# Graph attention and routed FFN on one core: POOL's gathers take their cue from TensorE's steps

## What is computed

```
xn   = layernorm(x);  xp = (xn @ W) as 4 heads x 64
alpha = leaky_relu(a_src[src] + a_dst[dst])
w    = softmax of alpha over the edges of each target (with a loop edge)
x    = x + elu(segment_sum(xp[src] * w, dst) + bias)
xn   = layernorm(x);  r = xn @ wr + br
y    = (gelu(xn @ w1 + b1) @ w2 + b2) * r    for the K = 6249 nodes of largest r, in one choice over all nodes
x    = x + xn  (every node), + y (chosen nodes)
```

## Time and profile before

| | us |
|---|---|
| median of 3 runs | 3182.54 (3172.71 to 3183.56) |
| the profiled execution's own time | 3182.05 |
| its span, first to last instruction | 3180.3 |
| PE busy | 2095.3 (66%) |
| POOL busy | 1596.4 (50%) |
| DVE busy | 1597.0 (50%) |
| ACT busy | 722.8 (23%) |
| mean granted clock of TensorE | 0.789 of full speed |
| DMA | 365.42 MB, 115 GB/s over the span |

### The profile page before, as it was taken

One profiled execution on the slowest core, in us unless ns is written; L12 is line 12 of the kernel. 1 busy time (PEld: TensorE's weight loads), 2 busy tenths in 40 slices (PEclk: granted clock), 3 DMA queues, 4 the chain that ended last, 5 costly groups with the idle time before them and its releaser, 6 DMA issues.

```text
span 3180.3 us, 39382 instructions
## 1 busy us (share of the span) xinstructions
PE 2095.3 (66%) x10886; PEld 1777.2 (56%) x10887; DVE 1597.0 (50%) x3933; ACT 722.8 (23%) x1899; POOL 1596.4 (50%) x1675
## 2 busy tenths in 40 slices
PE   8646766657666666676676666766657567676675
PEld 6535655546556555565555555655556555565564
DVE  7654545444454454544544545445445454454556
ACT  5301221212212222122121221221212212122123
POOL 3465545455454554545545545455455454554530
PEclk9867878777787787777877878778778787787788
DMA  7643333333333333333333333333333333333329
GB/s 244 189 123 106 106 104 105 102 105 107 102 106 104 105 104 104 105 103 108 103 103 102 110 99 106 104 105 101 105 103 105 106 102 102 99 109 101 107 72 318
DMA packets 216050, 365.42 MB, mean 115 GB/s; under 512 B 62102, under 2 KB 151346, under 8 KB 216019
## 3 DMA queue, kind: packets, MB, share of 16 engines
q0 software_dynamic: 77488, 214.85, 25.7%
q1 hardware_dynamic: 124434, 136.80, 14.0%
q10 hardware_dynamic: 14096, 13.41, 1.2%
HBM read 326.04 MB, written 38.89 MB: 115 GB/s over the span
## 4 chain that ended last, share of the span: by engine, by line
PE 62%; issue 33%; DVE 3%; DMA 0%; ACT 0%; DVEq 0%; ACTq 0%; SPq 0%
PE ag_ps L939 28%; PE h_ps L909 15%; PE y_ps L922 10%; PE lk_ps L890 3%; PE tr_ps L898 2%; PE ag_ps L831 2%; PE ag_ps L952 1%; DVE base L1442 1%; DVE st_b L1056 0%; PE y_ps L924 0%; DMA node_rows<-base 0%; DVE rows L1250 0%; PE tr_ps L854 0%; PE xl_ps L854 0%; DVE rows L1046 0%
## 5 line engine op out<-in xcount | busy, mean ns | idle before, releaser
L637 POOL DMA_INDIRECT rows<-node_rows,ends x1613 | 1555.6, 964 | 1393.8 <-PE ag_ps L939 908.7
L909 PE MATMUL h_ps<-xnT,w1s 128*128 128x128 f32 x3136 | 488.5, 286 | 818.1 <-issue 818.0
L939 PE MATMUL ag_ps<-rows,oh 128*128 128x260 f32 x3322 | 946.2, 454 | 31.2 <-issue 23.2
L909 PEld LDWEIGHTS h_ps<-xnT,w1s 128*128 128x128 f32 x3136 | 421.5, 199 | 820.1 <-issue 808.7
L939 PEld LDWEIGHTS ag_ps<-rows,oh 128*128 128x128 f32 x3322 | 759.0, 232 | 180.9 <-issue 33.6
L1300 DVE SCALAR_TENSOR_TENSOR base<-steps_of_rows 128x256 f32 (+1 forms) x98 | 42.0, 429 | 1365.8 <-ACT steps_of_rows L790 1365.8
L1250 DVE TENSOR_TENSOR rows<-rows,xl_ps 128x768 f32<-128x768 f32 (+2 forms) x685 | 495.6, 793 | 29.1 <-ACT xl_ps L750 18.1
L721 ACT COPY xnT<-tr_ps 128x256 f32<-128x256 f32 x98 | 36.7, 374 | 1428.9 <-PE tr_ps L898 1337.3
L922 PE MATMUL y_ps<-w2s,hT 128*128 128x256 f32 x1568 | 355.4, 379 | 1.6 <-ACT hT L731 1.6
L922 PEld LDWEIGHTS y_ps<-w2s,hT 128*128 128x128 f32 x1568 | 297.4, 190 | 42.5 <-issue 1.8
L1212 DVE TENSOR_TENSOR oh<-xl_ps,dloc 128x2176 f32<-128x2176 f32 x98 | 236.9, 2418 | 0.0
(11 more groups left out here) (206 smaller groups left out, 1380.0 us busy)
## 6 DMA issues: line engine op xcount, KB each, us to landing
dbc<-dst SPq DMA_DIRECT2D x97, 544.0 KB
rows<-node_rows,ends POOLq DMA_INDIRECT x1613
selfr<-node_rows SPq DMA_DIRECT2D x98, 130.0 KB
base<-in_x SPq DMA_DIRECT2D x14, 896.0 KB, 5.8
base<-in_x SPq DMA_DIRECT2D x49, 256.0 KB
ffn_rows<-yb ACTq DMA_DIRECT2D x96, 128.0 KB, 1.7
node_rows<-base SPq DMA_DIRECT2D x13, 910.0 KB, 5.8
out<-base SPq DMA_DIRECT2D x3, 1024.0 KB, 9.2
```

Source lines behind the costliest of these rows:

```text
L637: pool.indirect_dma_start(out=rows[:, b, t, :], out_offset=None, in_=table, in_offset=bass.IndirectOffsetOnAxis(ap=ends[:, b, t, 0:1], axi ...
L909: last = nc.tensor.matmul(h_ps[:, m * P:(m + 1) * P], w1s[:, c, m * P:(m + 1) * P], xnT[:, c, :], start=(c == 0), stop=(c == DC - 1))
L939: product = nc.tensor.matmul(ag_ps[b][:, 0:ROW], oh[:, b, t, :], rows[:, b, t, :], start=(t == 0), stop=False)
```

## The change

POOL no longer waits for `freed` of block w-2. In block w (from w = 1 on) it waits, ahead of gather 4, for the look-ups of block w (`lk_ok`); ahead of gathers 8, 11 and 13, for the three groups of sums of block w-1 (`freed[0]`, `freed[1]`, `freed[2]`); and ahead of gather 16, for the second FFN layer of block w-4, which PE does behind the sums of block w-1 (`y_ok`). Gather 0 waits for `ends` alone. That the products of block w-2 are done before gather 0 of block w follows from the wait ahead of gather 13 in block w-1. POOL's loop has its first two turns written out instead of one. Apart from this, SP waits for `y_ok` and loads the "ffn" rooms ahead of the first store of `out` rather than behind it.

```diff
+    LOOKED_UP, SUMMED, SECOND_LAYER = 4, (8, 11, 13), TILES - 1
...
             sp.wait_ge(y_st[1], 16 * (PAIRS - 1))
+            sp.wait_ge(y_ok, NW)
+            load_free("ffn")
             for c, (first, count, _) in enumerate(ends_with):
...
-                if c == 0:
-                    sp.wait_ge(y_ok, NW)
-                    load_free("ffn")
...
+            def follow(w, t):
+
+                if t == LOOKED_UP:
+                    wait_apart(pool, (lk_ok, w + 1))
+                for k in range(GROUPS):
+                    if t == SUMMED[k]:
+                        wait_apart(pool, (freed[k], w))
+                if t == SECOND_LAYER and known(w, 4):
+                    wait_apart(pool, (y_ok, w - 3))
+
...
                 for t in range(last):
-                    if known(w, 2) and t % FREED == 0:
-
-                        wait_apart(pool, *([(ld_ends[b], 32 * (i + 1))] if t == 0 else []), (freed[t // FREED], w - 1))
+                    if known(w, 2) and t == 0:
+                        wait_apart(pool, (ld_ends[b], 32 * (i + 1)))
+                    if known(w, 1):
+                        follow(w, t)
                     gather(t, gath[b])
+                if known(w, 1):
+                    follow(w, last)
...
-            two_by_two(pool, PAIRS, window, last_peeled=True)
+            two_by_two(pool, PAIRS, window, last_peeled=True, first_peeled=2)
```

## The result

| | before | after |
|---|---|---|
| median, us | 3181.79 (3172.71 to 3183.56, 4 runs) | 2711.39 (2703.0 to 2718.25, 4 runs) |
| ratio, 95% interval | | 0.8528 [0.8502, 0.8555] |
| profiled execution, us | 3182.05 | 2703.0 |
| its span | 3180.3 | 2701.2 |
| granted clock | 0.789 | 0.844 |

Faster by 470 us, where 202 were forecast. The time lies outside the range (2740 to 3200) and nearest to the rival "the crawl nearly goes" (2738).

What follows compares the result with a forecast made beforehand. The bound was a ring of POOL's gathers and PE's work, 30.8 us a block; 93 periods at -2.1 us give -195, start -5 and end -2.4, so 3182 - 202 = 2980 us, range 2740 to 3200.

Steps and rivals of the forecast that it cites:

- the crawl nearly goes: Rival: almost nothing left for PE after its slow stretch; -4.7 us a block, 2738 us; chance 0.13.
- the crawl: PE's slow stretch while POOL gathers: one pair of weight load and matmul per 2.1 us, against 0.12 before.
- The ring and the stock: Steady block: 21.0 us gathers, 2.8, then 7.0 of PE's work; during gathers PE lives on some 60 held pairs.
- another cause, tied to PE's place: Rival: PE's slowness comes from its place, not from held pairs; no change, about 3180 us; chance 0.13.
- one pause, and inner waits that cost nothing: POOL idles some 7 us ahead of gather 4; later waits end before POOL arrives, 0.1 us a block.
- -5.4 + 0.1 + 2.8 + 0.4 = -2.1: Us a block: POOL's earlier start, later waits, PE's pairs left, turn wholly behind the slow stretch; block of 28.7 us.
- The 13 pairs left behind the crawl: PE's load-and-matmul pairs still to do before turn and look-ups: +2.8 us a block, bounds 0.2 to 5.3.
- the fast rival: The rival "the crawl nearly goes": 2738 us, chance 0.13.
- Late rows: Block's last gather lands at about 18 us after the look-ups; DVE waits 5 us more, hidden by 9 us of cover.
- Gathers beside the load: Gathers 4 to 7 run beside SP's 544 KB load of targets: taken as 0, bound 1.9 us a block.
- Start and end: Start: POOL lets PE go on in block 2's look-ups, some -5 us; end: earlier ffn loads, -2.4 us.

Runs made afterwards that it cites:

- sums_end_only_b: Changed kernel with only the wait ahead of gather 13, for the last group of sums, left in the loop; 1.0701 of the kernel before, 3432 us.
- half_hidden_b: Kernel before with 16 of the first FFN layer's 32 matmuls left out in the loop; 0.9709 of the kernel before.
- half_gathers_c: Kernel before with every second gather of the loop's blocks left out; 0.643 of the kernel before, 2045.8 us.
- more_waits: Changed kernel with five more waits a block that never hold, for look-ups long done; 0.8503 of the kernel before.

## Why the prediction was wrong

**The ring and the stock.** Right as a description. Two kernels that it wasn't made for, sums_end_only_b and half_hidden_b, come out of the ring within 0.6 us, and these and half_gathers_c fall into the 51 to 62 pairs. The rival "another cause, tied to PE's place" is refuted by half_hidden_b. What the stock is made of is not shown. I read it as instructions that PE holds and that run out. But in the kernel before PE's updates are late well before its pairs are: all 120 recorded for matmuls that end up to 5 us behind POOL's start are on time, all 491 for those that end 7 to 22 us behind it are over 1 us late, and the pairs turn slow only at 11.3 us. The eight updates for the 32 matmuls of the first layer in the earlier trace rows, which began at 1518.61, stand at 1534.78 to 1535.19, 0.06 us apart, when PE was back at speed. So it can as well be reports or records that PE has to get rid of and that pile up. The Trainium skill, "Runtime: NRT & Kernel Launch", section "Instruction fetch mechanics", says that the cost of fetching ahead is mostly hidden as long as no branch leaves what was fetched; these blocks are a loop, with one branch back for every two. Chip B agrees (no idle before the first layer); on the others PE stood 818.0 us there, but no run shows that fetching is what was late.

**The step that failed: one pause, and inner waits that cost nothing.** I put POOL's pause ahead of gather 4 at some 7.7 us and took 0.1 us for all the other waits, since they "end before POOL gets there". That holds for the matmuls only: in 96 of the 103 pauses they had ended before the pause began. What a wait waits for is the semaphore's update, and beside running gathers it comes up to 11.8 us behind the matmul (6.5 at the median), 2.0 us behind the last gather. So the inner waits do hold, and each pause is some 2.8 us. The row that I took for what a wait costs, at most 0.3 us between gathers, came from waits that held nothing, as those of more_waits. In the kernel before nothing showed it, as POOL's own updates there are on time; the late ones, of the second layer by 13.1 us and of the first by 13.5 at the median, held nobody up. The sum "-5.4 + 0.1 + 2.8 + 0.4 = -2.1" became 25.35 - 30.37 = -5.0 us a block. The long pause of 9.8 us, in which PE had to do 7 us of work first, is gone; in its place are 1.7 short ones that end as soon as the gathers have stopped and an update for work long done arrives.

**The 13 pairs left behind the crawl (+2.8 us).** They come from the same step. A block has 104 pairs (85 and the turn's and look-ups' 19); with one refill of some 55 and 10 that trickle in, about 39 are left, for which POOL must stand still for long. With two short pauses PE gets two refills. Then the block is POOL's again: 20.5 us and about 1.8 times 2.8. The two refills are worked out from these counts; no run changes the number of refills alone.

**The rival that came true.** "If short pauses at the waits for sums refill the stock" is what happened, and -4.7 us was its price. I gave it only 0.13 because the waits would end early; the matmuls that they name do, their updates don't.

**Late rows.** "9 us of cover" was wrong in size and hid itself: the sums of 1507.08 follow gathers of 1496 to 1502 and DVE's `zz` at 1505.20 within 1.9 us, and PE stood 6.97 us. PE's idle before the sums rose from 31.2 to 354.3 us. I take it to cost little, as POOL is the bound by then, but no run removes it; on chip B the same wait is there (3.54 us).

**Gathers beside the load.** Taken at 0, bound 1.9 us a block: the 1613 gathers took 1556.9 us in all against 1555.6. Right, though the two gathers of the earlier trace rows were a thin sample: of the first seven, from 136.73 on, five took 1.1 to 1.6 us.

**Start and end.** -2.4 us for the end, -2.9 measured, in an interval that reaches to 0. The 5 us at the start were not measured by themselves.

**Chances.** 0.73 for faster was right in sign. The range ended at 2740 because the gain of the fast rival was tied to a reason I held for improbable; the floor that the profile did show, 20.95 us of gathers a block (3182 - 93 x 9.1 = 2336 us), should have stretched it further.

## What to carry to other kernels

When an engine stands for "issue", count its instructions from one known event to the stop, in several places; if the count agrees and the time doesn't, something that it holds a fixed number of has run out or filled up. Don't take the end of an instruction for the moment at which its semaphore is raised: compare the end of the wait with the update of the semaphore, and the update with the instruction. Splitting one long pause of the gathering engine into two short ones, so that each refill of the others is used, was worth 15% here, though the engine's own work grew by nothing. A wait's price can't be read from waits that never hold.

## What the runs showed of the hardware

Chips differ: the same kernel before took 2277 us on one chip and 3182 to 3210 on the others. On that one neither the crawl nor a late update of PE occurs.

On the others, while indirect gathers are under way, TensorE starts a pair of load and matmul only about every 2.1 us once 51 to 62 pairs are used up, and its updates of semaphores come late, by up to 11.8 us in the changed kernel. Both come back 1.7 to 3.0 us behind the last gather, at the same moment (1495.17 and 1495.20).

What in the chip or around it differs stays open. One rival is untested: the recording of the trace may itself take part, since the chips with the crawl are those whose traces lack records of updates (3,735 of landed rows in before against 24,991 on chip B), and every execution on record has a recorded clock beside it, so none shows the kernel without recording.
